# A masked attention loop entered with 14 row products, query spreads in its steps, an earlier self-attention tail, and a front without identity products

## The chip, the cores and the metric

The kernel runs on one core of a Trainium2 chip. The metric is the device time of one execution in microseconds (us). Engines are named as in the profile: PE (TensorE, matrix products and transposes), DVE (VectorE), ACT (ScalarE), POOL (GpSimd) and SP (the queue that issues the DMAs). Every engine works through its own list of instructions in order. An instruction may wait for a semaphore that another engine raises.

## The reference, cut to what matters

Two decoder layers on x of shape (2, 256, 128), each followed by a residual sum and a layernorm. The change touches the first two parts of the second layer: a self-attention with rotary positions (16 heads of 8), and a masked cross-attention to a context of 512 rows (16 heads of 8).

```
x = _layernorm(x + _L0_attn_ref(x, ...))            # state-space mixer
x = _layernorm(x + _L0_xattn_ref(x, ctx_1024, ...)) # cross-attention, 16 heads of 64
x = _layernorm(x + _L0_ffn_ref(x, ...))             # 8 experts
x = _layernorm(x + _L1_attn_ref(x, ...))            # "a" in the kernel
x = _layernorm(x + _L1_xattn_ref(x, ctx_1024, ctx_1024, mask, ...))  # "x" in the kernel
x = _layernorm(x + _L1_ffn_ref(x, ...))             # 32 experts

def _L1_attn_ref(x, ...):
    ...
    attn = jnp.einsum('bhqd,bhkd->bhqk', query, key) / scale
    attn = jax.nn.softmax(attn, axis=-1)
    out = jnp.einsum('bhqk,bhkd->bhqd', attn, value)
    return out.transpose(0, 2, 1, 3).reshape(b, s, d_model) @ Wo_w + Wo_b

def _L1_xattn_ref(query, key_, value, mask, ...):
    ...
    logits = jnp.einsum('bhsd,bhtd->bhst', q, k)
    logits = jnp.where(mask[:, None, :, :], jnp.float32(-100000000.0), logits)
    score = jax.nn.softmax(logits, axis=-1)
    attn = jnp.einsum('bhst,bhtd->bhsd', score, v) / jnp.sqrt(jnp.float32(D_HEAD))
    return jnp.einsum('bhsd,hdo->bso', attn, Wo) + bo
```

## The kernel before

The program is one list per engine, written out by hand with semaphores. The batch has two entries, 0 and 1, of 256 rows. Every attention of layer 1 (`L` is "a" for self-attention, "x" for the masked one) has three pieces.

**Spreads.** Queries and keys are kept as three bf16 parts. A spread is a set of products with a selection matrix (`sel_s`, `sel_k`) that writes the parts of some heads, stacked, into PSUM; ACT copies them to `qs` or `ks`. Its operand is gathered first from the parts by 32-row copies (`gather_four`) on POOL, DVE or ACT; the table `GATHERED` says which engine does which. In "a" there are 16 spreads (`SPREADS`), of keys and queries of both entries, each with 4 products on PE (`spread_a`) and a copy of 128x1024 on ACT. In "x" there are 16 spreads of queries alone (8 per entry), each with 2 products (`spread_x`) and a copy of 128x512 on ACT. The keys of "x" come over DMA.

**The front (`first_slots`, `fill_slot`).** The softmax needs each row's maximum before its exponentials. A row product (`rows`) fills one PSUM bank with 128 query rows by 512 logits; DVE takes the maximum of it (`row_max`), in "x" with the mask in the same instruction. When a group of heads is done, a "max" slot transposes the maxima on PE (`max_cols`), ACT negates them (`minus_max`), POOL splits them in three parts (`minus_parts`) and SP writes these with three DMAs into `qs` (`spread_max`), so that the second set of logits comes out with the maximum already taken off. A slot may only be filled when its bank's slot before it has been read (`before_in_bank`, `used`): a row slot by DVE, a max slot by ACT, that is by `minus_max`. `AHEAD` says how many row products are made before the loop: 16 of 32 for "a", 18 of 64 for "x". `idle_work(bank, n)` makes n products of the identity with itself, whose result nobody reads; `fill_slot` makes 2 ahead of every row product of the front of "a", and 1 in the front of "x".

**The loop.** 16 steps for "a", 32 for "x". In step n PE makes the logits of step n + 1 (`logits`), the products with the values of step n (`values`), and the slots that `slots_beside(L, n)` puts there: up to three row products, or two and a max. ACT takes the exponentials of step n, 128x1024 (`exp_late`). `logits` of a group's first step waits for that group's maxima to have landed (`a_nm_stack`, `x_nm_stack`). In "x" groups are of 4 heads, there are 8 groups, and group k is first needed by the logits of step 4k, which PE makes in step 4k - 1.

**The tail.** For an entry that is finished, PE turns the output to rows (`out_rows`), DVE divides by the sums (`normed_rows`), PE turns back (`attended_cols`) and multiplies by the output weight (`attended_rows`), DVE adds the residual (`a_summed`) and, once POOL has the reciprocal root (`root`), scales (`a_scaled`). The next part starts with a transpose (`half_cols`), the query product of "x" (`queries`) and the split of it (`query_parts`, DVE). `TURNED` and `BESIDE` say in which step of the loop each piece of entry 0 is done; entry 1's come after the loop, or in the front of "x" after the row product named by `SECOND`. Between the loop of "a" and the front of "x" PE goes through `out_rows`, `queries(0)`, `attended_cols(1)`, `attended_rows(1)`, 8 identity products, and `spread_x` 0 and 1, in this order (`attend_x`).

POOL's list around the front of "x" is: the root of post3_0, the gather of entry 0's second quarter, the root of post3_1, the gathers of entry 0's third and fourth quarter, a residual sum, the three gathers of entry 1, and only then `minus_parts("x", 0)` and the others.

## Time and profile before

| | us |
|---|---|
| median of 3 runs | 469.82 |
| lowest, highest | 468.88, 471.14 |
| the profiled execution | 467.58 |
| its span in the trace | 465.8 |
| front of "a" (first row product to first logits) | 33.1 |
| loop of "a", to the copy of its last output | 29.2 |
| from there to the first row maximum of "x" | 6.4 |
| front of "x" | 16.3 |
| loop of "x" | 65.5 |
| rest, to the end | 44.9 |

The last six rows are stretches of the span, cut at 270.4, 303.5, 332.7, 339.1, 355.4 and 420.9 us. The span begins some 2 us after the execution does. A time in the trace is the start of a row, counted from the start of the span. A row of PE's timeline stands for a run of equal products; each product of f32 operands counts as two passes, so that 1 identity product shows as "x2".

### The profile page before, as it was taken

The page shows a single profiled execution, that of the slowest core. Times are in us where ns is not written, and L with a number is a line of the kernel's source. Part 1 is how long each engine was busy: PE and PEld are TensorE (multiplying, and loading weights), DVE is VectorE, ACT ScalarE, POOL GpSimd, SP SyncE. Part 2 cuts the span into 40 slices and gives each one's busy share as a digit, 9 for nine tenths or more (in the row PEclk, how much of TensorE's full clock was granted, in tenths as well). Part 3 has the DMA queues.
Part 4 walks back from the last instruction along what each step waited for, and adds up shares of the span by engine and source line. Part 5 has one row for each costly group of instructions (what it writes and reads, how often), then busy time and mean ns, then how long its engine had stood idle before and what let it go on. Part 6 is the DMA issues. An engine that isn't in the chain of part 4 may idle for free.

```text
span 465.8 us, 7837 instructions
## 1 busy us (share of the span) xinstructions
PE 421.6 (91%) x2952; PEld 283.1 (61%) x2960; DVE 294.9 (63%) x688; ACT 206.2 (44%) x290; POOL 185.9 (40%) x237
## 2 busy tenths in 40 slices
PE   4898989999999999789999986979869999999985
PEld 4686645454545547466899875735546555667975
DVE  4779976767766665532522967555689887246744
ACT  1676623333333332034224364546447444566550
POOL 3326646887777775210222437133154322200000
PEclk9989999999999999899999997989999999999999
DMA  8712000000004111160153015100000000001000
GB/s 287 305 37 77 1 0 2 1 1 0 1 1 180 46 45 46 55 226 0 69 80 45 2 20 69 21 1 4 1 0 3 3 2 3 2 4 32 1 0 24
DMA packets 8081, 19.80 MB, mean 43 GB/s; under 512 B 1958, under 2 KB 3974, under 8 KB 7526
## 3 DMA queue, kind: packets, MB, share of 16 engines
q1 hardware_dynamic: 8044, 19.30, 14.3%
q8 instruction: 24, 0.39, 0.4%
q14 instruction: 13, 0.11, 0.1%
HBM read 17.26 MB, written 1.15 MB: 40 GB/s over the span
## 4 chain that ended last, share of the span: by engine, by line
PE 69%; DVE 15%; issue 5%; POOL 5%; ACT 4%; DMA 1%; another core or an unknown queue 0%; SPq 0%; POOLq 0%; DVEq 0%; ACTq 0%
PE ps L1667 67%; DVE ps L1412 3%; DVE big L1216 2%; POOL big L695 2%; DVE ps L1211 1%; DMA ident<-in_ident 1%; POOL big L702 1%; ACT late L968 1%; DVE big L1288 1%; PE ps L1679 1%; DVE mx_a L1416 1%; POOL big L651 1%; PE ps L2116 1%; ACT big L894 0%; ACT late L1062 0%
## 5 line engine op out<-in xcount | busy, mean ns | idle before, releaser
L1667 PE MATMUL ps<-big,late 128*32 128x256 f32 (+3 forms) x760 | 96.4, 382 | 2.1 <-DVE mx_a L1416 0.9
L1667 PE MATMUL ps<-late,big 128*128 128x128 f32 (+1 forms) x448 | 65.6, 277 | 2.3 <-ACT late L968 1.3
L955 ACT ACTIVATE big<-ps 128x1024 f32<-128x1024 f32 x48 | 49.1, 1024 | 39.0 <-PE ps L1667 38.7
L894 ACT ACTIVATE big<-ps 128x1024 f32<-128x1024 f32 x32 | 32.8, 1024 | 65.2 <-PE ps L1667 56.8
L1667 PEld LDWEIGHTS ps<-late,big 128*128 128x128 f32 (+1 forms) x448 | 47.2, 152 | 20.0 <-issue 13.2
L1667 PEld LDWEIGHTS ps<-big,late 128*32 128x32 f32 (+2 forms) x768 | 35.4, 116 | 38.3 <-issue 18.5
L695 POOL TENSOR_TENSOR big<-big 128x512 f32<-128x512 f32 x32 | 41.0, 1284 | 28.1 <-DVE big L1288 28.1
L1288 DVE TENSOR_SCALAR big<-big 128x1024 f32<-128x1024 f32 x32 | 27.7, 865 | 33.2 <-ACT big L894 33.2
L1412 DVE CUSTOM_DVE_ANT_0 ps<-ps,big 128x512 f32<-128x512 f32 x64 | 42.7, 708 | 6.9 <-remote 3.2
L1667 PE MATMUL ps<-ident 128*128 128x128 f32 x268 | 39.6, 291 | 7.4 <-DMA ident<-in_ident 6.9
L630 POOL TENSOR_SCALAR vareps<-meanvar 128x2 f32<-128x2 f32 (+2 forms) x13 | 3.0, 228 | 104.5 <-DVE meanvar L1110 100.8
L1667 PEld LDWEIGHTS ps<-ident 128*128 128x128 f32 x268 | 36.6, 207 | 8.5 <-DMA ident<-in_ident 6.9
L917 ACT ACTIVATE big<-ps 128x512 f32<-128x512 f32 x32 | 18.9, 598 | 34.0 <-PE ps L1667 34.0
L1667 PE MATMUL ps<-ctx_r,attn_w 128*128 128x512 f32 x64 | 32.6, 618 | 0.7 <-ACT late L861 0.7
L1416 DVE TENSOR_REDUCE mx_a<-ps 128x2 f32<-128x512 f32 x32 | 21.1, 689 | 16.8 <-PE ps L1667 16.7
L1667 PE MATMUL ps<-xT,late 128*128 128x256 f32 (+1 forms) x96 | 29.9, 452 | 1.2 <-ACT big L917 1.2
L1667 PE MATMUL ps<-attn_w,ctx_r 128*128 128x128 f32 (+1 forms) x192 | 29.5, 287 | 0.4 <-ACT late L968 0.3
L1667 PE MATMUL ps<-attn_w,big 128*128 128x128 f32 x192 | 26.5, 285 | 2.9 <-DVE big L1280 2.3
L1279 DVE RECIPROCAL big<-ps 128x256 f32<-128x256 f32 x16 | 28.0, 1748 | 1.3 <-PE ps L1667 1.3
L1667 PEld LDWEIGHTS ps<-attn_w,ctx_r 128*128 128x128 f32 (+1 forms) x192 | 23.7, 171 | 7.4 <-issue 2.8
L651 POOL TENSOR_TENSOR big<-big,mid 128x512 f32<-128x512 f32 x16 | 20.4, 1274 | 19.7 <-DVE big L1216 19.7
L1667 PEld LDWEIGHTS ps<-attn_w,big 128*128 128x128 f32 x192 | 24.3, 197 | 5.9 <-DVE big L1280 2.8
(261 smaller groups left out, 728.3 us busy)
## 6 DMA issues: line engine op xcount, KB each, us to landing
attn_w<-in_w_x SPq DMA_DIRECT2D x1, 2560.0 KB, 12.9
big<-parts_kx SPq DMA_DIRECT2D x18, 128.0 KB
late<-in_w_up SPq DMA_DIRECT2D x1, 2048.0 KB, 8.5
late<-in_w_dn SPq DMA_DIRECT2D x4, 512.0 KB, 4.0
attn_w<-in_w_up SPq DMA_DIRECT2D x1, 1024.0 KB, 7.6
attn_w<-in_w_dn SPq DMA_DIRECT2D x1, 1024.0 KB, 9.8
big<-mid SPq DMA_DIRECT2D x24, 32.0 KB, 1.8
parts_kx<-ctx_r SPq DMA_DIRECT2D x1, 768.0 KB, 3.2
```

The costliest lines, as they stand in the source:

```text
L651: nc.gpsimd.tensor_tensor(hC[:, s % 8, :], hs[:, s % 4, :], Cn[:], ALU.mult).then_inc(S["hC_done"], 1)
L695: nc.gpsimd.tensor_tensor(esum[:, s, :].rearrange("p (r t) -> p r t", r=2), e[:, :, 0, :], e[:, :, 1, :], ALU.add).then_inc(S["e0_sum"], 1)
L702: nc.gpsimd.tensor_tensor(etot[:, b, :], esum[:, 0, :], esum[:, 1, :], ALU.add).then_inc(S["e0_tot"], 1)
L894: nc.scalar.activation(ex[:, n % 3, :].rearrange("p (r n) -> p r n", r=2), ps[:, 2 * (n % 2):2 * (n % 2) + 2, :], ACT.Exp).then_inc(S["e0_ ...
L917: nc.scalar.activation(dst, ps[:, up_bank0(k, c), :], ACT.Gelu).then_inc(S["up0_act"], 1)
L955: nc.scalar.activation(ex1[:, n % 3, :].rearrange("p (r n) -> p r n", r=2), ps[:, 2 * (n % 2):2 * (n % 2) + 2, :], ACT.Exp, scale=scale).t ...
L1216: nc.vector.tensor_tensor_scan(hs[:, s % 4, :], dA[:, s % 2, :], dBx, 0.0, ALU.mult, ALU.add).then_inc(S["scan_done"], 1)
L1279: link(nc.vector.reciprocal(dst, ps[:, 4 + b, T:2 * T]))
L1288: nc.vector.tensor_scalar(ex[:, n % 3, :], ex[:, n % 3, :], float(np.exp(CLIP)), float(np.exp(-CLIP)), ALU.min, ALU.max).then_inc(S["e0_cl ...
L1412: nc.vector.tensor_tensor_reduce(ps[:, bank, :], ps[:, bank, :], mq[:, 2 * b + q, :], 1.0, -FAR, ALU.add, ALU.max, dst).then_inc(S[f"{L}_r ...
L1416: nc.vector.tensor_reduce(dst, ps[:, bank, :].rearrange("p (h k) -> p h k", h=heads), AX.X, ALU.max).then_inc(S[f"{L}_redmax"], 1)
L1667: return nc.tensor.matmul(o, lhsT, rhs, start=start, stop=stop, skip_group_check=shared)
```

## The change

1. `AHEAD["x"]` goes from 18 to 14. Four row products move from the front of "x" into its loop. The max slot of a group is placed after the first row product of the next group, no longer after its second.
2. The 8 spreads of entry 1's queries leave the front of "x". `later_slots` adds one to each of the first 8 steps of the loop, as the last slot of the step. ACT's copy of it comes after the exponentials of the step. `spreads_x` spreads entry 0 beside rows 1, 3, 5, 7, 9 and 11.
3. `BESIDE["x"]` and `TURNED["x"]` come one or two steps later, to follow the row products.
4. Entry 0's tail of "a" comes one step earlier (`TURNED` 9 to 8, "aT" 11 to 10, "y" 12 to 11); its scaling goes from step 15 to step 13, its transpose `half_cols` to step 14 and `queries(0)` to step 15. `query_parts(0)` stands ahead of `normed_rows("a", 1)` on DVE.
5. In the front of "x", `queries(1)` follows row product 4 instead of 3, and `query_parts(1)` follows maximum 8 instead of 5.
6. In the front of "a" identity products go from 48 to 11. Entry 1's spreads are ordered keys first, and spreads 8 to 11 stand together ahead of row product 8. `values_a` comes last.

```diff
-        SPREADS = [(kind, b, f) for b in range(B)
-                   for kind, f in (("k", 0), ("k", 1), ("q", 0), ("k", 2), ("q", 1), ("k", 3), ("q", 2), ("q", 3))]
+        SPREADS = ([(s[0], 0, int(s[1])) for s in ("k0", "k1", "q0", "k2", "q1", "k3", "q2", "q3")]
+                   + [(s[0], 1, int(s[1])) for s in ("k0", "k1", "k2", "k3", "q0", "q1", "q2", "q3")])
...
-        AHEAD = {"a": 16, "x": 18}
+        AHEAD = {"a": 16, "x": 14}
...
-                if L == "x" and m % row_steps(L) == 1 and m > 1:
+                if L == "x" and m % row_steps(L) == 0 and m:
                     slots.append(("max", m // row_steps(L) - 1))
...
+                if L == "x" and n < H // 2:
+                    slots.append((n, ("spread", H // 2 + n)))
...
-        TURNED = {"a": 9, "x": 19}
-        BESIDE = {"a": {"aT": 11, "y": 12}, "x": {"aT": 20, "y": 21, "xT": 24, "router": 25}}
+        TURNED = {"a": 8, "x": 21}
+        BESIDE = {"a": {"aT": 10, "y": 11, "xT": 14}, "x": {"aT": 22, "y": 23, "xT": 25, "router": 26}}
...
-            return [m - 2] if 8 <= m < AHEAD["x"] else [2 + m // 2] if m % 2 else []
+            return [2 + m // 2] if m % 2 and m < H - 4 else []
...
-        SECOND = {"xT": 1, "q": 3, "parts": 5}
+        SECOND = {"xT": 1, "q": 4, "parts": 8}
...
+                    for (kind, i), bank in slots_beside("x", n):
+                        if kind == "spread":
+                            spread_x(i, bank)
...
+                query_parts(0)
                 normed_rows("a", 1, 1.0)
...
-            query_parts(0)
             a_summed(1)
...
                     if slot == ("row", 8):
-                        spread_a(8)
-                        spread_a(9)
-                        idle_work(1, 16)
-                        spread_a(10)
-                    fill_slot("a", slot, bank, 2)
+                        idle_work(2, 8)
+                        for n in (8, 9, 10, 11):
+                            spread_a(n)
+                    fill_slot("a", slot, bank, 1 if slot in (("row", 0), ("row", 1), ("row", 8)) else 0)
...
+                    if n == BESIDE["a"]["xT"]:
+                        half_cols("a", 0)
+                    if n == BESIDE["a"]["xT"] + 1:
+                        queries(0)
```

Three places show what the tables do. The first is PE in the loop of "x", around the max slot of group 1. In the kernel before it is the last slot of the front: `mx_x` is the maxima, `neg_i` the mask product that belongs to the logits, a 128x512 product is a row product, and `fours` gathers are waited for by a spread.

```order
L2039 MATMUL ps<-ident,mx_x 4x128 [waits x_redmax]
L2039 MATMUL ps<-ident,mx_x 4x128
L1667 MATMUL ps<-late,big1 128x256 [waits x_nm_stack0]
L1667 MATMUL ps<-late,big1 128x256
L1667 MATMUL ps<-sel,neg_i 128x256 x2
L1667 MATMUL ps<-late,big1 128x256 x2
L1667 MATMUL ps<-sel,neg_i 128x256 x2
L1667 MATMUL ps<-big1,late 128x512 [waits x_redmax,x_spread]
```

In the changed kernel the same slot stands in step 1, with a spread behind it.

```order
L2046 MATMUL ps<-ident,mx_x 4x128 [waits x_redmax]
L2046 MATMUL ps<-ident,mx_x 4x128
L1672 MATMUL ps<-attn_w,ctx_r 128x256 [waits fours_dve,x_redmax]
L1672 MATMUL ps<-attn_w,ctx_r 128x256
L1672 MATMUL ps<-big2,late 32x256 [waits x_e_exp]
L1672 MATMUL ps<-big2,late 32x256 x3
L1672 MATMUL ps<-big1,late 128x512 [waits x_spread,nm_ps]
L1672 MATMUL ps<-late,big1 128x256 [waits x_e_exp]
```

The row product that opens the next step now waits for `nm_ps` (`minus_max` on ACT); the same holds behind the max slots of groups 2 and 3.

The second place is ACT in the loop of "x", from its first exponentials (128x1024) on. Before:

```order
L955 ACTIVATE big2<-ps 128x1024 [waits x_s_ps] x3
L955 ACTIVATE big2<-ps 128x1024 [waits x_e_used,x_s_ps]
L1012 ACTIVATE mid<-ps 4x256 [waits x_nm_done,x_mT_ps]
L955 ACTIVATE big2<-ps 128x1024 [waits x_e_used,x_s_ps] x3
L1012 ACTIVATE mid<-ps 4x256 [waits x_nm_done,x_mT_ps]
```

And in the changed kernel:

```order
L957 ACTIVATE big2<-ps 128x1024 [waits x_s_ps]
L1005 ACTIVATE late<-ps 128x512 [waits x_spread_ps]
L957 ACTIVATE big2<-ps 128x1024 [waits x_s_ps]
L1005 ACTIVATE late<-ps 128x512 [waits x_spread_ps]
L957 ACTIVATE big2<-ps 128x1024 [waits x_s_ps]
L1014 ACTIVATE mid<-ps 4x256 [waits x_mT_ps]
L1005 ACTIVATE late<-ps 128x512 [waits x_spread_ps]
```

A spread's copy now stands between any two of the first exponentials, and `minus_max` (4x256) behind both.

The third place is DVE at the end of the loop of "a". `COPY mid` keeps an output, `rden` and `x2` are `normed_rows`, `ctx_r`, `cv` and `attn_w` are `query_parts`. Before:

```order
L1442 COPY mid<-ps 128x256 [waits a_e_used,norm_out]
L1425 RECIPROCAL rden<-ps 128x16 [waits a_oT_ps]
L1425 RECIPROCAL rden<-ps 128x16
L1429 SCALAR_TENSOR_TENSOR x2<-ps,rden 128x128 [waits dve_own]
L1429 SCALAR_TENSOR_TENSOR x2<-ps,rden 128x128
L1133 TENSOR_SCALAR ctx_r<-ps,vec 128x256 [waits qk_ps]
```

And in the changed kernel:

```order
L1447 COPY mid<-ps 128x256 [waits a_e_used]
L1138 TENSOR_SCALAR ctx_r<-ps,vec 128x256 [waits qk_ps]
L1140 SCALAR_TENSOR_TENSOR cv<-ps,vec,ctx_r 128x256 [waits x_q_parts]
L1141 CAST ctx_r<-cv 128x256 [waits dve_own]
L1143 TENSOR_TENSOR ctx_r<-cv,ctx_r 128x256 [waits x_q_parts]
L1150 COPY attn_w<-ctx_r 32x256 [waits x_q_parts]
L1150 COPY attn_w<-ctx_r 32x256 x2
L1430 RECIPROCAL rden<-ps 128x16 [waits a_oT_ps]
```

The split of the queries now lies ahead of `normed_rows`, for whose result PE waits before it goes on to the spreads of "x". POOL's and SP's lists are the same in both kernels.

## Rows read from the trace of the kernel before

**Rows 1.** Stretches: PE, PEld, DVE, ACT, POOL; clock, DMA, GB/s.
```profile
270.40:303.50 33.10, 26.59 (x203) 23.35 (x201) 20.48 (x38) 17.03 (x22) 14.45 (x28) 0.90 0.29 39
...
339.10:355.40 16.30, 12.12 (x86) 8.99 (x85) 14.98 (x44) 8.59 (x16) 9.56 (x21) 1.00 0.00 0
355.40:420.90 65.50, 63.25 (x595) 36.12 (x599) 42.16 (x143) 35.75 (x43) 15.63 (x30) 1.00 0.03 9
```
**Rows 2.** PE's timeline in the front of "a": start, duration, [idle before, releaser].
```profile
279.60 0.38 PE L2039 MATMUL ps<-ident,mx_a 128*8 128x128 f32 x2 [0.88 <-DVE mx_a L1416]
...
285.36 1.89 PE L1667 MATMUL ps<-big,ctx_r 96*128 96x256 bf16 x8 [3.89 <-ACT big L945]
287.04 5.10 PE L1667 MATMUL ps<-ident 128*128 128x128 f32 x32
...
303.50 1.86 PE L1667 MATMUL ps<-late,big 128*128 128x256 bf16 x8 [1.31 <-ACT late L968]
```
**Rows 3.** DVE's timeline there: row maxima of "a".
```profile
293.28 1.36 DVE L1416 TENSOR_REDUCE mx_a<-ps 128x2 f32<-128x512 f32 x2 [4.27 <-PE ps L1667]
```
**Rows 4.** POOL's timeline there: the key gathers of entry 1.
```profile
284.07 4.41 POOL L730 COPY big<-ctx_r 32x256 bf16<-32x256 bf16 x9 [1.14 <-DVE ctx_r L1138]
```
**Rows 5.** DVE's timeline at the end of the loop of "a".
```profile
332.30 0.43 DVE L1442 COPY mid<-ps 128x256 f32<-128x256 f32 x1 [0.69 <-PE ps L1667]
333.25 0.37 DVE L1425 RECIPROCAL rden<-ps 128x16 f32<-128x16 f32 x2 [0.53 <-PE ps L2116]
...
334.06 0.48 DVE L1133 TENSOR_SCALAR ctx_r<-ps,vec 128x256 bf16<-128x256 f32 x1
...
335.88 1.02 DVE L1145 COPY attn_w<-ctx_r 32x256 bf16<-32x256 bf16 x3
```
**Rows 6.** PE's timeline there: entry 1's tail, identity products, first spreads of "x".
```profile
334.20 0.44 PE L2125 MATMUL ps<-ident,x 128*128 128x128 f32 x2 [0.50 <-DVE x L1429]
...
335.66 1.95 PE L1667 MATMUL ps<-ident 128*128 128x128 f32 x16
337.44 0.60 PE L1667 MATMUL ps<-attn_w,ctx_r 96*128 96x256 bf16 x4
```
**Rows 7.** POOL's timeline, front of "x": gathers of entry 1's queries.
```profile
346.83 4.05 POOL L730 COPY attn_w<-ctx_r 32x256 bf16<-32x256 bf16 x9 [3.39 <-DVE ctx_r L1138]
```
**Rows 8.** PE's timeline, loop of "x": logits, max slots, a row product.
```profile
355.36 0.38 PE L1667 MATMUL ps<-late,big 128*128 128x256 bf16 x2
...
368.52 0.38 PE L2039 MATMUL ps<-ident,mx_x 128*4 128x128 f32 x2
...
370.06 0.38 PE L1667 MATMUL ps<-big,late 128*128 128x512 bf16 x1
370.28 0.38 PE L1667 MATMUL ps<-late,big 128*128 128x256 bf16 x2
...
375.11 0.38 PE L2039 MATMUL ps<-ident,mx_x 128*4 128x128 f32 x2
```
**Rows 9.** DVE's timeline there: the masked maximum of that row product.
```profile
370.48 0.70 DVE L1412 CUSTOM_DVE_ANT_0 ps<-ps,big 128x512 f32<-128x512 f32 x1
```
**Rows 10.** ACT's timeline: a spread's copy, exponentials and `minus_max`, step after step.
```profile
355.33 0.60 ACT L1003 ACTIVATE late<-ps 128x512 bf16<-128x512 f32 x1 [0.43 <-PE ps L1667]
...
362.13 1.02 ACT L955 ACTIVATE big<-ps 128x1024 f32<-128x1024 f32 x1 [1.17 <-PE ps L1667]
363.05 0.36 ACT L1012 ACTIVATE mid<-ps 4x256 f32<-4x256 f32 x1
```
**Rows 11.** ACT's last `minus_max` of "a", and PE's wait for its DMA.
```profile
320.79 0.36 ACT L1012 ACTIVATE mid<-ps 8x256 f32<-8x256 f32 x1
```
**Rows 12.** PE's timeline: the logits that wait for it.
```profile
325.46 0.60 PE L1667 MATMUL ps<-late,big 128*128 128x256 bf16 x4 [0.33 <-DMA late<-mid]
```
**Rows 13.** Two stretches, columns as in Rows 1.
```profile
283.00:290.00 7.00, 4.64 (x23) 4.21 (x24) 5.68 (x14) 3.37 (x5) 5.19 (x13) 0.51 0.55 70
344.50:351.30 6.80, 4.15 (x31) 3.07 (x32) 6.61 (x20) 3.45 (x7) 3.90 (x10) 1.00 0.00 0
```

More of the change, by code:

```diff
@@ L984, in attend_a @@
                 gather_four(1)
-                for n in range(8, 15):
+                for n in range(8, 16):
                     spread(n)
                 minus_max("a", 1, dict(first_banks("a"))["max", 1])
-                spread(15)
                 for n in range(B * (H // 4) * KEYS["a"] // P):
@@ L2016, in used @@
                     pe.wait_ge(S[f"{L}_redmax"], i + 1)
+                elif kind == "spread":
+                    pe.wait_ge(S["x_spread"], i + 1)
                 else:
@@ L2064, in fill_slot @@
                     rows(L, i, bank)
+                elif kind == "spread":
+                    spread_x(i, bank)
                 else:
@@ L2173, in attend_a @@
                         spread_a(7)
+                    if slot == ("row", 6):
                         front_products(1)
@@ L2176, in attend_a @@
                         latent_products(1)
-                    if slot == ("row", 9):
-                        spread_a(11)
-                    if slot == ("row", 11):
-                        spread_a(12)
-                    if slot == ("row", 13):
-                        spread_a(13)
-                        values_a()
-                    if slot == ("row", 15):
-                        spread_a(14)
+                    if slot in (("row", 9), ("row", 11), ("row", 13)):
+                        spread_a(12 + (slot[1] - 9) // 2)
                 spread_a(15)
+                values_a()
                 for slot, bank in slots_beside("a", None)[-2:]:
@@ L2202, in attend_a @@
                         out_rows("a", 1, range(H // 4 - 1))
+                    if n == BESIDE["a"]["xT"]:
+                        half_cols("a", 0)
+                    if n == BESIDE["a"]["xT"] + 1:
+                        queries(0)
                     values("a", n)
@@ L2209, in attend_x @@
                 total = B * (H // 4) * KEYS["x"] // P
-                half_cols("a", 0)
                 out_rows("a", 1, (H // 4 - 1,))
-                queries(0)
                 attended_cols("a", 1)
```

5 lines of the change are left out of this document (2 added, 3 removed).

## The prediction, made before the changed kernel was run

> **What bounds the kernel now.** I read four views: the stretches of the span with each engine's busy time, the timelines of PE, DVE, ACT and POOL where the change works, the waits with their releasers, and the order of the instructions. The stretches [rows 1] show two kinds of place. In the loop of "x" PE is busy 63.25 of 65.5 us, so whatever is put in PE's list there is paid in full, and every new wait too. In the two fronts PE is busy 80% and 74%. What sets their length is read from the timelines: chains through DVE, ACT and POOL, and in "a" also the identity products. Nothing ahead of 270 us or behind the loop of "x" is touched, so the four stretches between carry the whole sum.
>
> **Front of "a": shorter by 7.3 us.** PE reaches the first max slot at 279.60 [rows 2]. The 16 identity products ahead of it cost 3.5 us of PE. DVE needs 8 maxima at 0.65 (1.36 for two that overlap a little, [rows 3]), the scaling of entry 1's x (0.6), and a wait for row product 7 behind `front_products` (some 0.9), which makes 6.7 from 271.1. The slot comes 1.9 us earlier, at 277.7. From there to 285.36 the chain runs through the key split and ACT's gather (the 3.89 of idle time, [rows 2]), and it moves along by 1.9: spread 8 starts at 283.4. The 8 identity products now lie in PE's idle time and cost nothing; without that cover they would cost 1.8. Spreads 9 to 11 wait for POOL's key gathers, 4.41 for the three [rows 4], which end at 288.5 now and at 286.6 then. Row product 8 goes out at 287.2 and DVE starts on it at 287.65, where it starts at 293.28 now [rows 3]; before, 16 identity products ran from 287.04 to 291.98 [rows 2]. Eight maxima take 5.2, to 292.9. Then come the max slot, spread 15, `values_a` (1.1) and DVE's addition of it (0.7): first logits at 295.4 where they are at 303.50 [rows 2], 8.1 less. I take 7.3. The reason is the clock: from 283 to 290 the granted clock is 0.51, the level of 1.2 GHz, after a stretch with PE idle for 3.9 us; from 344.5 to 351.3 it is full with PE busy 61% [rows 13]. [...] At the low level a pair of row products and a spread costs PE 1.76, not 0.88, against DVE's 1.3; that is 0.46 for each of four pairs. Bounds: 6.0 and 8.1.
>
> **The tail: longer by 3.0 us.** Step 8 still waits for the last `minus_max` of "a" and the logits of step 12 for its DMA [rows 11, 12], so the earlier `out_rows` moves little. `half_cols(0)` stands in step 14 and waits for the scaling, some 0.4 of wait; ACT copies it ahead of the exponentials of step 15, and the values of step 15 end 0.65 late. The last output is kept at 333.4, not at 332.73 [rows 5]. Then DVE does `query_parts(0)` and its gather first, 334.06 to 336.90 or 2.84 [rows 5], and only then `normed_rows`, after which PE starts `attended_cols(1)` 0.95 later (333.25 to 334.20, [rows 5, 6]). That gives 337.2 where it is 334.20. The earlier split gains nothing, since in PE's list the spreads of "x" stand behind this transpose. All behind it moves by 3.0: the identity products at 335.66, the first spreads at 337.44 [rows 6].
>
> **Front of "x": longer by 1.8 us.** It has fewer products, but they are not what ends it. POOL's gathers of entry 1's queries end at 350.88 [rows 7], and `minus_parts("x", 0)` is behind them. From the end of a `minus_max` to the logits that need it are 4.31 (321.15 to 325.46, [rows 11, 12]), so 350.88 gives 355.19, and the first logits are at 355.36 [rows 8]. With `query_parts(1)` behind maximum 8 instead of 5, POOL starts three maxima, 2.0, later. The slack of 0.2 is used up, and 1.8 is left. The four row products, 8 spreads and the max slot that leave this front were beside that chain; their removal is worth nothing here.
>
> **Loop of "x": longer by 10.9 us.** Three steps take 6.59 (368.52 to 375.11), one 2.20; a row product takes 0.22 of issue (370.06 to 370.28, [rows 8]). Of the 2.20, row products are 0.66, logits 0.88 and the rest, the values, 0.66.
> - A step with three row products and a spread: the spread uses bank 7, where the second row product went. That is issued at 0.66, DVE starts 0.42 later (370.06 to 370.48) and takes 0.70 [rows 8, 9], so the spread is issued at 1.85 and not at 1.54. With 0.22 and 0.66 behind it the step is 2.73, or 0.53 more. Five such steps: 2.7. Lower bound: the 0.22 of issue alone, 1.1.
> - A step with a max slot (1, 4 and 7): the slot uses bank 6, and the next step opens with a row product in bank 6, which waits for `minus_max`. ACT takes the spread's copy first (0.60), from 2.27 to 2.87, then exponentials (0.92 until the next may start) and `minus_max` (0.36) [rows 10]: 4.15 from the step's start, and the row product at 4.2, not at 2.2. Three times 2.0 is 6.0. Before, the waiting row product was the second of its step and no spread's copy stood ahead of the exponentials.
> - Group 1's maxima are needed by the logits of step 4, made in step 3. `minus_max` ends at 4.15 of step 1, plus 4.31 makes 8.5; PE is there at 4.2 + 2.73 + 0.22 = 7.15. Another 1.3.
> - The four row products from the front land in steps that had none: 0.9.
>
> Together 10.9. No row shows a spread inside this loop, so both ends stay: 2.7 if only the issue is paid (8 spreads and 4 row products at 0.22), 12 if values and DVE slip too.
>
> **Clock at the two new gaps: 1.2 us longer.** PE is idle from 333.7 to 337.2 ahead of `attended_cols(1)`, and some 4 us ahead of the first logits of "x" (counted from the first maximum of "x": the last one ends at 13.9, after 7.8 for the first nine, 2.8 for the split and its gather and 3.3 for five more; the logits are at 16.3 + 1.8 = 18.1). The nearest row is the gap of 3.89 before 285.36, after which the clock stayed at 0.51 until 290 [rows 2, 13]. If both fall, the 8 identity products and the entry of the loop run at half speed and cost up to 5; if neither, nothing. The Trainium skill (TensorE: Matmul & The Clock Gate, "What's actually happening") states that the throttled clock is the default and that activity releases it; by that rule, which the 0.51 behind the gap agrees with, taking identity products out of a sparse front is no free gain. It is the rival below and not in this sum.
>
> **The sum.** -7.3 + 3.0 + 1.8 + 10.9 + 1.2 = +9.6. The profiled execution took 467.58, which gives 477.2. The median of the three runs is 2.2 above it, and the forecast goes by the median: 469.8 + 9.6 = 479.4. The forecast's own range: -8.1, +3.0, +1.6, +8.3 and 0 at the low end, 474.6; -6.0, +3.2, +2.0, +12 and +5 at the high end, 486.
>
> **Rivals.** (1) The clock stays low: the front of "a" saves 5, the 8 identity products cost 1.8 more, and the masked loop's entry 2.5 more. With 3.0, 1.8, 10.9 and 0.9 for the max steps that run partly at half speed the sum is about +15, 485. For it: the two low stretches of this trace, each behind a sparse stretch. Against: 344.5 to 351.3 stayed full. (2) The waits in the masked loop cost half, because ACT is ahead there (idle 1.17 before each exponential, [rows 10]) and takes copies sooner: +5.5 instead of +10.9, -8.1 in front, no clock cost, +2.2, 472.0. (3) Faster: `minus_max` is done before the next row product needs its bank. That decides between 0.66 after the max slot (no wait) and the 2.8 that I count. Then the loop costs 2.7, the front saves 8.1, the low clock at the entry of the loop of "a" goes too (1.6), and the tail and the front of "x" still cost 4.8: -2.2, 467.6. Against it stands ACT's own list, in which the copy of the step's spread and the exponentials are ahead. (4) The front of "a" does not shorten as told, since it waits for POOL's gathers: it saves 4, and the time is 483.
>
> **How the numbers follow.** Chances: forecast 0.64, rival 1 0.16, rival 2 0.09, rival 3 0.06, rival 4 0.05. The predicted time is the forecast's, 479.4. The range 471.5 to 486 takes in the forecast's own range, rivals 1 and 4, and rival 2. A measurement of this kernel can tell about 0.5% from no change, 2.3 us. Faster (below 467.5): 0.04, half of rival 3 and a little. Same: 0.07, the rest of rival 3 and half of rival 2. Slower: 0.89.
>
> **What would show it.** First logits of "a" some 7 to 8 us earlier in the span; `attended_cols(1)` with a long wait for DVE and `query_parts(0)` ahead of it; first logits of "x" 18 us after the first masked maximum, not 16.3; in the first 8 steps of the masked loop a PE timeline with three waits of 1.5 to 2 us on `minus_max` and one on a DMA, 27 to 28 us for the 8 steps instead of 17.6; the granted clock under 1 in at least one more stretch. The prediction fails if PE meets no `nm_ps` wait there, or if the identity products that went had kept the clock up.

## The result, and the profile after

The changed kernel takes 479.99 us (median of 4 runs, 477.43 to 480.71), the kernel before 470.48 in the same comparison (468.88 to 471.32). The ratio is 1.0196, 95% interval 1.0148 to 1.0245: slower by 9.5 us, where 479.4 was forecast. The profiled execution took 479.72. The one of the kernel before took 467.58, 2.9 under the median here, so the two traces stand 12.1 us apart and the medians 9.5. Three executions of the whole study fell into a slow state (480.69 us of the kernel with `minus_max` first, 707.03 of the one with the split back behind `normed_rows`, 1059.26 of the kernel before) and are in none of the medians or ratios.

The page of the changed kernel, its head, the busy times and the granted clock in 40 slices:

```profile
span 477.9 us, 7691 instructions
...
PE 418.8 (88%) x2870; PEld 273.5 (57%) x2878; DVE 294.5 (62%) x688; ACT 205.1 (43%) x290; POOL 185.6 (39%) x237
...
PEclk9999999999999999899999988998959999999998
```

PE does 2.8 us less and the span is 12.1 us longer. The time is in waits. The three stretches that answer to [rows 1] (same columns), front of "a", front of "x", loop of "x":

```profile
269.70:296.50 26.80, 20.54 (x128) 13.69 (x127) 20.00 (x38) 16.95 (x22) 13.87 (x28) 0.87 0.31 47
337.30:354.60 17.30, 9.22 (x55) 6.52 (x53) 12.54 (x37) 4.34 (x8) 7.71 (x17) 0.83 0.00 1
354.60:434.70 80.10, 71.23 (x623) 40.03 (x630) 45.78 (x153) 39.77 (x51) 15.58 (x30) 0.97 0.03 7
```

The last stretch runs to the transpose of the routing weights (434.67). Counted to the same transpose (422.51) before the change it is 67.2 us long, so it grew by 12.9.

**Front of "a".** PE's timeline (start, duration, [idle before, releaser]): max slot 0, spread 8, row product 8, max slot 1, first logits. [Rows 2] has the same places.

```profile
277.00 0.38 PE L2046 MATMUL ps<-ident,mx_a 128*8 128x128 f32 x2 [0.87 <-DVE mx_a L1421]
...
282.77 1.16 PE L1672 MATMUL ps<-big,ctx_r 96*128 96x256 bf16 x8 [1.91 <-ACT big L947]
...
287.19 1.06 PE L1672 MATMUL ps<-big,late 128*128 128x256 bf16 x4
...
293.66 0.38 PE L2046 MATMUL ps<-ident,mx_a 128*8 128x128 f32 x2 [0.89 <-DVE mx_a L1421]
...
296.51 1.03 PE L1672 MATMUL ps<-late,big 128*128 128x256 bf16 x8 [0.94 <-DVE late L1476]
```

The first logits are 7.0 us earlier. Of this 0.7 was there before the front began (its first product is at 269.7, not 270.4), 1.9 falls ahead of the first max slot and 4.4 behind it: 6.3 net.

**The loop of "a".** One wait in it is longer than before: the logits of step 12 wait 1.89 us for their DMA, where it was 0.33 [rows 12].

```profile
319.05 0.60 PE L1672 MATMUL ps<-late,big 128*128 128x256 bf16 x4 [1.89 <-DMA late<-mid]
```

Nine of the traced kernels have the moved steps of the tail. In three of them (the changed kernel and the two in the section on the tail) this wait is 1.64 to 1.89 us, in the other six none is recorded. In the five kernels without the moved steps it is 0.32 or 0.33. So it is a matter of the execution; whether the moved steps make it likelier is not shown.

**The tail.** DVE keeps the last output, splits entry 0's queries, gathers, and only then takes up `normed_rows` (the reciprocal). PE's two rows are `attended_cols(1)` and the 8 identity products.

```profile
326.76 0.42 DVE L1447 COPY mid<-ps 128x256 f32<-128x256 f32 x1 [2.37 <-PE ps L1672]
327.11 0.47 DVE L1138 TENSOR_SCALAR ctx_r<-ps,vec 128x256 bf16<-128x256 f32 x1
...
328.92 1.02 DVE L1150 COPY attn_w<-ctx_r 32x256 bf16<-32x256 bf16 x3
329.97 0.37 DVE L1430 RECIPROCAL rden<-ps 128x16 f32<-128x16 f32 x2
```
```profile
330.92 0.44 PE L2134 MATMUL ps<-ident,x 128*128 128x128 f32 x2 [3.24 <-DVE x L1434]
...
332.85 2.97 PE L1672 MATMUL ps<-ident 128*128 128x128 f32 x16
```

PE stands still for 3.24 us, where it was 0.50 [rows 6], and the identity products behind take 2.97, not 1.95. DVE's reciprocal starts 3.21 behind the copy of the last output (326.76 to 329.97), where it was 0.95 (332.30 to 333.25, [rows 5]): 2.26 more. The copy itself is late too. From the last max slot of "a" to it are 12.33 us before the change (319.97 to 332.30) and 13.20 in the trace of the tail alone and in those of five other kernels that have the moved steps and no late DMA: 0.87 more. (The changed kernel needs 14.98, with 1.78 for the late DMA.)

**Front and loop of "x".** PE's timeline: the first logits; the max slot of step 1; the row product of bank 6 that opens step 2 (its row carries the name of the logits); the logits of group 1; the spreads of steps 5 and 6.

```profile
354.64 0.61 PE L1672 MATMUL ps<-late,big 128*128 128x256 bf16 x2 [3.03 <-DMA late<-mid]
...
361.44 0.38 PE L2046 MATMUL ps<-ident,mx_x 128*4 128x128 f32 x2
...
364.48 0.38 PE L1672 MATMUL ps<-late,big 128*128 128x256 bf16 x2 [1.50 <-ACT mid L1014]
...
368.34 0.38 PE L1672 MATMUL ps<-late,big 128*128 128x256 bf16 x2 [0.91 <-DMA late<-mid]
...
376.96 0.39 PE L1672 MATMUL ps<-attn_w,ctx_r 96*128 96x256 bf16 x2 [0.20 <-DVE mx_x L1417]
...
379.75 0.39 PE L1672 MATMUL ps<-attn_w,ctx_r 96*128 96x256 bf16 x2 [0.20 <-DVE mx_x L1417]
```

The 1.50 on `mid` is the wait for `minus_max`; it stands again at 375.30 and 385.01. From the max slot to the row product behind it are 3.04 us (361.44 to 364.48). A step with three row products and a spread takes 2.79 (376.96 to 379.75). The first eight steps take 28.7 (356.32 to 385.01). ACT's timeline beside the first of the three waits: the spread's copy, the exponentials, and `minus_max` behind both, ready to run since the max slot at 361.44:

```profile
362.44 0.60 ACT L1005 ACTIVATE late<-ps 128x512 bf16<-128x512 f32 x1 [1.41 <-PE ps L1672]
362.94 1.02 ACT L957 ACTIVATE big<-ps 128x1024 f32<-128x1024 f32 x1
363.84 0.36 ACT L1014 ACTIVATE mid<-ps 4x256 f32<-4x256 f32 x1
```

### The profile page after: what moved, and what is told of

Its sections match the earlier page's. It is cut to its first block, busy times and chain, and to the rows that moved or that the text cites. A ratio compares the mean times of both kernels' runs of the same rounds, so it can differ in the third digit from the quotient of the medians.

```text
span 477.9 us, 7691 instructions
## 1 busy us (share of the span) xinstructions
PE 418.8 (88%) x2870; PEld 273.5 (57%) x2878; DVE 294.5 (62%) x688; ACT 205.1 (43%) x290; POOL 185.6 (39%) x237
## 4 chain that ended last, share of the span: by engine, by line
PE 61%; DVE 15%; POOL 7%; issue 6%; ACT 5%; DMA 3%; SPq 1%; another core or an unknown queue 1%; POOLq 0%; DVEq 0%; ACTq 0%
PE ps L1672 59%; DVE ps L1417 3%; POOL big L697 2%; DVE mx_a L1421 1%; DMA late<-mid 1%; DVE big L1221 1%; SPq L560 1%; DVE ps L1216 1%; DMA big<-mid 1%; DVE big L1293 1%; POOL big L732 1%; POOL big L704 1%; POOL attn_w L732 1%; DMA ident<-in_ident 1%
## 5 line engine op out<-in xcount | busy, mean ns | idle before, releaser
L1672 PE MATMUL ps<-big,late 128*32 128x256 f32 (+3 forms) x760 | 97.5, 383 | 2.9 <-DVE mx_a L1421 1.8
L1672 PE MATMUL ps<-ident 128*128 128x128 f32 x186 | 29.0, 307 | 9.5 <-DMA ident<-in_ident 5.7
L1672 PEld LDWEIGHTS ps<-ident 128*128 128x128 f32 x186 | 27.4, 222 | 10.5 <-DMA ident<-in_ident 5.7
L744 POOL CAST mid<-mid 4x256 bf16<-4x256 f32 (+1 forms) x12 | 4.6, 387 | 64.5 <-ACT mid L1014 64.4
L1672 PE MATMUL ps<-attn_w,big 128*128 128x128 f32 x192 | 25.5, 279 | 2.9 <-DVE big L1285 2.3
L1672 PEld LDWEIGHTS ps<-attn_w,ctx_r 128*128 128x128 f32 (+1 forms) x192 | 22.0, 162 | 10.6 <-DVE mx_x L1417 4.0
L1672 PE MATMUL ps<-big,mid 64*128 64x256 f32 x192 | 27.2, 402 | 0.0
## 6 DMA issues: line engine op xcount, KB each, us to landing
attn_w<-in_w_x SPq DMA_DIRECT2D x1, 2560.0 KB, 12.9
```

Of the source, the lines that this page charges most:

```text
L1672: return nc.tensor.matmul(o, lhsT, rhs, start=start, stop=stop, skip_group_check=shared)
```

## Each part of the change alone

Three kernels hold one part each. They and the fourth kernel were timed beside the kernel before, whose median was 470.76 (19 runs). The others were timed in two later sessions, in which it was 469.9 (22 runs) and 470.04 (17 runs). A ratio is always to the kernel before in the same session. It need not agree with the difference of two medians to better than 1 or 2 us, and where the two differ both are given.

The front of "a" alone. Its diff against the kernel before, cut:

```diff
-                        spread_a(8)
-                        spread_a(9)
-                        idle_work(1, 16)
-                        spread_a(10)
-                    fill_slot("a", slot, bank, 2)
+                        idle_work(2, 8)
+                        for n in (8, 9, 10, 11):
+                            spread_a(n)
+                    fill_slot("a", slot, bank, 1 if slot in (("row", 0), ("row", 1), ("row", 8)) else 0)
```

> The kernel before with only the new front of "a" (entry 1's key spreads first, no identity products ahead of rows 2 to 7 and 9 to 15, values_a last). Theory (the front's length is that of DVE's maxima, ACT's gather and POOL's gathers once the identity products are gone, 6.3 net in the trace of after): 6.3 us faster than before, about 464, with the first logits of "a" 7.0 us earlier in the span. Rival (most of it is given back in the loop of "a", whose DMA and exponentials set its end): 3 us faster or less.

Measured: 462.96 us, ratio 0.9845 (0.9808 to 0.9882), 7.8 us faster by the medians and 7.3 by the ratio. In its trace the first logits are at 297.35, 6.15 before those of [rows 2], and the span is 6.3 shorter. Nothing is given back behind them, so the rival falls.

The tail alone:

```diff
-        TURNED = {"a": 9, "x": 19}
+        TURNED = {"a": 8, "x": 19}
...
-        BESIDE = {"a": {"aT": 11, "y": 12}, "x": ...
+        BESIDE = {"a": {"aT": 10, "y": 11, "xT": 14}, "x": ...
...
+                query_parts(0)
                 normed_rows("a", 1, 1.0)
```

> The kernel before with only entry 0's tail moved one or two steps forward in the loop of "a" and its queries' split ahead of normed_rows on DVE. Theory (PE waits for normed_rows, which is 2.84 us later): 3 us slower than before, up to 4.5 with a low clock behind the longer gap; the transpose attended_cols(1) waits 3 us for DVE. Rival (the earlier split of the queries lets the front of "x" begin earlier, and what it costs on DVE it gives back): within 1 us of before.

Measured: 472.86 us, ratio 1.0059 (1.0035 to 1.0083), 2.1 us slower by the medians and 2.8 by the ratio. PE's `attended_cols(1)`:

```profile
337.63 0.44 PE L2126 MATMUL ps<-ident,x 128*128 128x128 f32 x2 [3.25 <-DVE x L1430]
```

The masked loop alone:

```diff
-        AHEAD = {"a": 16, "x": 18}
+        AHEAD = {"a": 16, "x": 14}
...
+                if L == "x" and n < H // 2:
+                    slots.append((n, ("spread", H // 2 + n)))
...
-        SECOND = {"xT": 1, "q": 3, "parts": 5}
+        SECOND = {"xT": 1, "q": 4, "parts": 8}
```

> The kernel before with only the masked loop's change (14 rows ahead of it, entry 1's query spreads in its first eight steps, queries(1) behind row 4, query_parts(1) behind maximum 8). Theory (PE is the bound there and gets 8 slots, three waits of 1.5 us and a DMA wait into its list, and the split comes three maxima later): 12 us slower than before, 11.7 from the loop and 1.1 from the front, less some 1 us if the clock stays full at the entry of the loop. Rival (part of the 12.7 in the trace of after comes from the low clock that the changed front and tail brought): 7 to 8 us slower.

Measured: 483.11 us, ratio 1.0271 (1.0237 to 1.0304), 12.4 us slower. The same waits are there without the new front and tail (the second row is the wait for group 1's maxima):

```profile
367.41 0.38 PE L1672 MATMUL ps<-late,big 128*128 128x256 bf16 x2 [1.50 <-ACT mid L1014]
...
371.29 0.38 PE L1672 MATMUL ps<-late,big 128*128 128x256 bf16 x2 [0.93 <-DMA late<-mid]
```

The rival falls as well: with the old front and tail the masked loop is 79.9 us long in the trace, and its entry is at the low clock all the same (0.59 from 357.8 to 361.8).

By the medians the three parts give -7.8 + 2.1 + 12.4 = +6.7, and together they measure +9.5. By the ratios they give -7.3 + 2.8 + 12.7 = +8.2, against +9.2. Each interval is 1 to 2 us either way, so the parts add as far as these runs can tell; whether they cost a little more together stays open.

## The masked loop: which wait, and why

ACT's order in the first eight masked steps, against the changed kernel:

```diff
-                    for (kind, i), bank in slots_beside("x", n - 1) if n else ():
+                    for (kind, i), bank in slots_beside("x", n - 1) if n > H // 2 else ():
                         if kind == "max":
                             minus_max("x", i, bank)
-                    for (kind, i), bank in slots_beside("x", n):
+                    for (kind, i), bank in slots_beside("x", n) if n < H // 2 else ():
+                        if kind == "max":
+                            minus_max("x", i, bank)
                         if kind == "spread":
                             spread_x(i, bank)
```

> The changed kernel, where ACT in the first eight masked steps takes minus_max of the step's max slot ahead of the copy of its spread and of the next exponentials, not behind both. Theory (the row product that opens the next step waits for minus_max behind those two): the three waits of 1.5 us go, 4.5 to 5 us faster than the changed kernel, about 475. Rival (ACT is as late with the exponentials instead, and PE waits for them): at most 1.5 us faster.

Measured: 474.6 us (8 runs), ratio to the kernel before 1.0087 (1.0054 to 1.012), 5.4 us faster than the changed kernel. ACT takes `minus_max` first, and PE's next wait is 0.16. The loop, first logits to the routing transpose, is 75.3 us, not 80.0. ACT and then PE at step 1:

```profile
359.62 0.37 ACT L1014 ACTIVATE mid<-ps 4x256 f32<-4x256 f32 x1 [0.78 <-PE ps L2048]
360.21 0.60 ACT L1005 ACTIVATE late<-ps 128x512 bf16<-128x512 f32 x1 [0.22 <-PE ps L1674]
360.70 1.02 ACT L957 ACTIVATE big<-ps 128x1024 f32<-128x1024 f32 x1
```
```profile
359.20 0.38 PE L2048 MATMUL ps<-ident,mx_x 128*4 128x128 f32 x2
...
360.90 0.38 PE L1674 MATMUL ps<-late,big 128*128 128x256 bf16 x2 [0.16 <-ACT late L1005]
...
364.15 0.38 PE L1674 MATMUL ps<-late,big 128*128 128x256 bf16 x2 [0.30 <-DMA late<-mid]
```

The exponentials lose nothing by it: they start 1.50 behind the max slot in both kernels (361.44 to 362.94, 359.20 to 360.70). The rival falls.

The spreads back in the front, still with 14 rows ahead:

```diff
-                if L == "x" and n < H // 2:
-                    slots.append((n, ("spread", H // 2 + n)))
...
-            return [2 + m // 2] if m % 2 and m < H - 4 else []
+            return {8: [6], 9: [7], 10: [8], 11: [9], 12: [10, 11], 13: [12, 13, 14, 15]}.get(m, [2 + m // 2] if m % 2 else [])
```

> The changed kernel with entry 1's query spreads back in the front of "x" (behind rows 8 to 13), still 14 rows ahead of the loop. Theory (the spreads lengthen five steps by 0.6 and, by the bank that they take, make the next step open with a row product that waits 1.5 us for minus_max, three times): 3.7 + 4.5 in the loop, less 1.3 that a longer wait for the DMA of group 1's maxima takes and 1 for the spreads in the front: 6 us faster than the changed kernel, 474. Rival (it is the four rows and the late max slots that cost, whoever else is in the step): at most 3 us faster.

Measured: 471.9 us, ratio 1.0057 (1.0022 to 1.0092), 8.1 us faster than the changed kernel by the medians, 6.5 by the ratios. The loop is 70.8 us. Its first logits, and those of group 1:

```profile
354.91 0.39 PE L1670 MATMUL ps<-late,big 128*128 128x256 bf16 x2 [0.20 <-DMA late<-mid]
...
364.93 0.38 PE L1670 MATMUL ps<-late,big 128*128 128x256 bf16 x2 [2.16 <-DMA late<-mid]
```

The spreads lie in what was the wait ahead of the first logits (0.20 here, 3.03 in the changed kernel). So of the 12.9 us that the loop grew, 9.2 go with the spreads (80.0 less 70.8). Not all of this is slots and waits: the entry of the loop is at full clock here (1.00 from 354.9 to 358.9) and at 0.50 in the changed kernel, and that costs 1.8, as the kernel with filled gaps below shows (78.2 against 80.0). The slots and waits that the spreads bring are thus 7.4. Of the 3.7 that are left the longest piece is the wait for group 1's maxima, which grew from 0.91 to 2.16 because PE reaches it sooner.

The front of "x" takes 17.39 us with the 8 spreads back in it and 17.36 without them (first masked maximum to first logits). Taking them out gained nothing there.

## The front of "x"

`queries(1)` and `query_parts(1)` as early as before, in the changed kernel:

```diff
-        SECOND = {"xT": 1, "q": 4, "parts": 8}
+        SECOND = {"xT": 1, "q": 3, "parts": 5}
```

> The changed kernel with queries(1) behind row 3 and query_parts(1) behind maximum 5, as before. Theory (POOL's gathers and minus_parts end the front of "x"): the first logits come 2 us earlier after the first masked maximum, 15.4 instead of 17.4, and the time is 478. Rival (the low clock or the wait for DVE's maximum ahead of row 12 ends the front): no change.

Measured: 480.33 us, ratio 1.0246 (1.0207 to 1.0285): 0.3 slower than the changed kernel by the medians and 2.3 by the ratios, with intervals that overlap. No gain is seen. Max slot 0 and the first logits:

```profile
349.69 0.38 PE L2046 MATMUL ps<-ident,mx_x 128*4 128x128 f32 x2 [3.48 <-DVE mx_x L1417]
...
355.37 0.61 PE L1672 MATMUL ps<-late,big 128*128 128x256 bf16 x2 [0.26 <-DMA late<-mid]
```

From `attended_cols(1)` to the first logits this trace needs 21.76 us (333.61 to 355.37), the changed kernel's 23.72 (330.92 to 354.64). So the 2.0 us are gained in the stretch, as the theory says, though the wait moves from the DMA to the max slot. The time doesn't show it. In the two profiled executions this kernel's first max slot of "a" is at 279.14, 2.1 us behind the changed kernel's 277.00, in a part where their instructions are the same, and its first logits of "a" wait 2.16 for a DMA, where the changed kernel's wait 0.94 for DVE. The trace bears the step out; the runs don't resolve it.

## The tail: order or steps

`query_parts(0)` back behind `normed_rows`, the moved steps kept:

```diff
-                query_parts(0)
                 normed_rows("a", 1, 1.0)
...
             attend_a()
+            query_parts(0)
             a_summed(1)
```

> The changed kernel with query_parts(0) back behind normed_rows of entry 1 on DVE; out_rows, attended_cols, half_cols and queries of entry 0 stay one or two steps forward. Tells DVE's order from the steps moved. Theory (normed_rows waits 2.84 us for the split and its gather, and nothing else of the tail costs): 2.8 us faster than the changed kernel, about 477, the wait ahead of attended_cols(1) falls from 3.24 us to about 0.5. Rival (the moved steps cost in the loop of "a" and the split is hidden): less than 1 us faster.

Measured: 477.0 us (4 runs), ratio 1.0137 (1.0106 to 1.0168), 3.0 us faster than the changed kernel by the medians and 2.8 by the ratios. DVE's reciprocal comes ahead of the split, and PE's wait is 0.98 (not 0.5: `queries(0)` filled the other half of it before, and now stands in the loop):

```profile
329.18 0.37 DVE L1430 RECIPROCAL rden<-ps 128x16 f32<-128x16 f32 x2 [0.53 <-PE ps L2125]
...
329.99 0.47 DVE L1138 TENSOR_SCALAR ctx_r<-ps,vec 128x256 bf16<-128x256 f32 x1
```
```profile
330.13 0.44 PE L2134 MATMUL ps<-ident,x 128*128 128x128 f32 x2 [0.98 <-DVE x L1434]
```

The steps moved forward, beside the new front of "a" and with DVE's old order. Against the kernel with that front alone, cut:

```diff
-        TURNED = {"a": 9, "x": 19}
+        TURNED = {"a": 8, "x": 19}
...
-        BESIDE = {"a": {"aT": 11, "y": 12}, "x": ...
+        BESIDE = {"a": {"aT": 10, "y": 11, "xT": 14}, "x": ...
...
+                    if n == BESIDE["a"]["xT"]:
+                        half_cols("a", 0)
+                    if n == BESIDE["a"]["xT"] + 1:
+                        queries(0)
```

> The kernel before with the new front of "a" and entry 0's steps moved forward, but with the split of the queries behind normed_rows (e1 and the half of e2 that is not DVE's order). Theory (the moved steps are neither late nor early for anyone, since PE's spreads stand behind attended_cols(1)): as e1, 463. Rival 1 (half_cols and queries out of the tail take 1 us off it): 462. Rival 2 (the wait for the scaling in the loop is paid): 464.

Measured: 463.41 us, ratio 0.9862 (0.9835 to 0.9889), against 462.96 and 0.9845 without them. The larger part of the tail's cost is DVE's order. That the moved steps cost nothing is not shown: the runs have 0.5 to 0.8, and in every trace that has them the last output of "a" is kept at least 0.87 late. The two rivals, 1 us to either side, can't be told from the theory by these runs.

## The front of "a": order, identity products, clock

The new order with two identity products ahead of every row product:

```diff
-                    fill_slot("a", slot, bank, 1 if slot in (("row", 0), ("row", 1), ("row", 8)) else 0)
+                    fill_slot("a", slot, bank, 2)
```

> The new front of "a" alone (as in e1), but with the two identity products ahead of every row product, as the kernel before has them. Tells the new order from the products that went. Theory (DVE's maxima at 0.65 set the pace of the second half, where two products a row are hidden; in the first half 12 products more cost 3.0 less 0.9 of idle time, some 2): 2 us slower than e1, 465; the order and the 16 products ahead of row 8 make the rest of the gain, some 5. Rival 1 (identity products cost as issued): 5 us slower than e1, near 468. Rival 2 (they keep the clock up, and its low stretches behind the gap go): as fast as e1 or 1 us faster.

Measured: 465.23 us, ratio 0.9942 (0.9909 to 0.9975), 2.3 slower than the front alone by the medians and 4.5 by the ratios. Its 12 runs fall in two groups, eight from 464.7 to 467.0 and four from 468.7 to 469.5; the profiled execution is of the second. In it max slot 0 is 2.1 later than in the front alone (279.75 against 277.67), max slot 1 is 5.8 later (299.74 against 293.98). Of the first, 1.9 is the 2 that was expected, and 0.2 was there before the front began. The other 3.7 were expected to be hidden. A part of the stretch between (columns as in [rows 1]):

```profile
288.70:295.00 6.30, 6.30 (x31) 5.48 (x32) 2.39 (x5) 2.73 (x3) 3.56 (x9) 0.52 0.32 48
```

PE is busy all of it, nearly all at the level of 1.2 GHz, so the products that hide beside DVE at full clock are paid here. Rival 2 falls: the identity products did not keep the clock up. Counted to the first logits, the front is 5.0 us longer (1.9 ahead of max slot 0 and 3.15 behind it), which is rival 1's size.

The whole span is 7.3 longer, and one piece of it is no cost of these products. The front of "x", which this kernel leaves as it was, takes 19.45 us against 16.28 in the front alone; its mean granted clock is 0.82 there, against 1.00. So the two groups of runs can't be read as theory and rival. A fairer comparison takes runs with the same mean granted clock of the whole execution: at 0.983 this kernel took 464.7 to 465.3 and the front alone 461.3, at 0.977 it took 468.7 to 469.5 and the front alone 462.8 to 465.6. With the 4.5 of the ratios, that speaks for rival 1 more than for the theory.

The gap ahead of spread 8 filled, in the kernel with the front of "a" alone:

```diff
-                        idle_work(2, 8)
+                        idle_work(2, 15)
                         for n in (8, 9, 10, 11):
```

> The new front of "a" alone (as e1) with 15 identity products ahead of spread 8 in place of 8, which fill most of the 1.91 us that PE waits there for ACT's gather. Theory (the low clock of the 3 to 4 us behind comes of PE standing still, and costs some 1.5 us there and at the entry of the loop of "a"): 1 to 2 us faster than e1, 461.5. Rival (DVE and POOL set this stretch, or the clock falls all the same): as e1, 463, or 0.5 slower.

Measured: 461.49 us, ratio 0.982 (0.9797 to 0.9843), against 462.96 and an interval that overlaps. It has the lowest median of the study. Max slot 0, spread 8 and first logits, here and then in the front alone:

```profile
275.58 0.38 PE L2038 MATMUL ps<-ident,mx_a 128*8 128x128 f32 x2 [0.88 <-DVE mx_a L1415]
...
281.34 1.15 PE L1666 MATMUL ps<-big,ctx_r 96*128 96x256 bf16 x8 [0.35 <-ACT big L945]
...
294.69 1.67 PE L1666 MATMUL ps<-late,big 128*128 128x256 bf16 x8 [0.94 <-DVE late L1470]
```
```profile
277.67 0.38 PE L2038 MATMUL ps<-ident,mx_a 128*8 128x128 f32 x2 [0.88 <-DVE mx_a L1415]
...
283.44 1.15 PE L1666 MATMUL ps<-big,ctx_r 96*128 96x256 bf16 x8 [1.91 <-ACT big L945]
...
297.35 1.87 PE L1666 MATMUL ps<-late,big 128*128 128x256 bf16 x8 [1.47 <-DMA late<-mid]
```

From max slot 0 to spread 8 both need 5.8 us: the products fill the gap and cost nothing. To the first logits it is 19.1 against 19.7. The clock still falls behind the gap (0.62 from 283.9 to 287.2). So 0.6 us is what the traces show in the front, and the rest of the 1.5 is not told apart from chance: all four runs have a mean granted clock of 0.983 or 0.984 and took 461.0 to 461.8, and the two runs of the front alone with 0.98 or more took 461.3 and 461.6.

## The clock at the two gaps

12 identity products ahead of `attended_cols(1)` and 12 ahead of the first logits of "x", in the changed kernel:

```diff
+                idle_work(2, 12)
                 attended_cols("a", 1)
...
+                idle_work(0, 12)
                 logits("x", 0)
```

> The changed kernel with 12 identity products (some 3 us at full clock) ahead of attended_cols(1), and 12 ahead of the first logits of "x", where PE waits for DVE and for a DMA. Theory (the gaps bring the granted clock to 0.5 for some 3 to 7 us behind them, which costs 1.4 at the tail and 2 at the entry of the masked loop): both low stretches go, 3 us faster than the changed kernel, about 477. Rival (what runs behind the gaps at half speed waits for DVE and ACT anyway): no change, or up to 1 us slower for products that don't fit in the gaps.

Measured: 478.27 us (475.14 to 481.11), ratio 1.0206 (1.0162 to 1.025) against the changed kernel's 1.0196: no difference can be told. The two stretches behind the gaps in the changed kernel, then in this one:

```profile
331.60:335.00 3.40, 3.17 (x15) 3.17 (x16) 1.16 (x5) 0.18 (x1) 0.43 (x2) 0.50 0.00 0
348.80:358.80 10.00, 6.01 (x23) 3.91 (x25) 3.48 (x10) 1.02 (x1) 3.67 (x8) 0.50 0.00 1
```
```profile
329.20:333.00 3.80, 3.33 (x28) 3.04 (x28) 1.16 (x5) 0.59 (x2) 0.73 (x2) 1.00 0.00 0
345.50:355.50 10.00, 7.34 (x59) 5.76 (x62) 4.35 (x14) 1.76 (x3) 3.84 (x9) 1.00 0.00 1
```

In the profiled execution the theory holds for the clock: the granted clock is 1.00 in both, the identity products behind the first gap take 1.95 again, and the loop is 78.2 us long, not 80.0. That execution is also the fastest of the six. The other five are as slow as the changed kernel, though the mean granted clock is higher in all six (0.976 to 0.987) than in the changed kernel's four (0.965 to 0.975). So the filled gaps raised the clock every time, and what that is worth in time is not shown; without a trace of the five it stays open. The Trainium skill (TensorE: Matmul & The Clock Gate, "What's actually happening") says that the throttled state is the default and that activity releases it. The one trace, with 1.00 behind both filled gaps, agrees.

## The changed kernel mended

`minus_max` first, entry 1's split early in the front of "x", entry 0's behind `normed_rows` in the tail. The diff is that of the fourth kernel with these lines:

```diff
-        SECOND = {"xT": 1, "q": 4, "parts": 8}
+        SECOND = {"xT": 1, "q": 3, "parts": 5}
...
-                query_parts(0)
                 normed_rows("a", 1, 1.0)
...
             attend_a()
+            query_parts(0)
```

> The changed kernel with three mends at once: minus_max ahead of the spread's copy (e4), queries(1) and query_parts(1) early (e7), and query_parts(0) behind normed_rows (e9). Theory (the three costs lie one behind the other and add): 5.3 + 2.0 + 2.8, so 10 us faster than the changed kernel, about 470, as the kernel before and 7 slower than e1. Rival (they overlap, or the wait for the first masked max slot and the low clock take the gain of e7): 473.

Measured: 469.25 us, ratio 0.9991 (0.9965 to 1.0017), 10.7 us faster than the changed kernel, as the theory said. The three mends one by one measured 5.4, -0.3 and 3.0, or 8.1; the sum of 10 needs the 2.0 that only the trace of the early split shows. So the costs add within the noise, and no closer. The masked loop as it is meant, with its worst waits gone (74.7 us), still takes back all that the front of "a" gains.

## Why the prediction was right, step by step

- **Front of "a", forecast -7.3:** right in mechanism, a little large. The trace has -6.3 net of an earlier start, the part alone -7.8 by the medians and -7.3 by the ratio. From max slot 0 to spread 8 it is 5.8 us (5.7 forecast), to row product 8 10.2 (9.5), from there to max slot 1 6.5 (some 5.8 at full clock) and on to the first logits 2.85 (some 2.4). That row product 8 stands at 287.19, with 287.2 forecast, is luck: the execution was 0.7 ahead. The four slow pairs at 0.46 add up to 1.8, and the forecast took 0.8 without saying why. Measured are 1.8 over its 17.7 at full clock, but at most 0.7 of that lies where those pairs are; the rest is in the pieces ahead of and behind them.
- **The tail, +3.0:** right in cause and size. Up to `attended_cols(1)` the tail's own cost is 3.13 in the traces: 0.87 for the moved steps (0.65 forecast) and 2.26 for the split ahead of `normed_rows`. The forecast's 2.84 is the whole split, but DVE had stood idle for 0.53 ahead of the reciprocal [rows 5], and that time takes up a part of it. The part alone costs 2.1 to 2.8, and undoing the order gives back 2.8 to 3.0.
- **Front of "x", +1.8:** right in cause; the stretch grew by 1.1 (16.30 to 17.36), and an early split brings 2.0 in the trace. The forecast took a chain that ends at POOL's last gather plus 4.31; that is what the trace has (350.57 to 354.64, 4.07). That the spreads taken out are worth nothing there is shown by putting them back.
- **Loop of "x", +10.9:** right. The trace has +12.9, and +11.1 when the clock is full at its entry (78.2 against 67.2). Its pieces: steps of 2.79 (forecast 2.73), three waits for `minus_max` of 1.50 behind exactly the instructions named (3.04 from max slot to row product, 2.8 forecast, and 0.66 by rival 3), and a wait of 0.91 for group 1's maxima (1.3). The eight steps take 28.7, of which 1.8 is the clock (27 to 28 forecast). Rival 3, that `minus_max` is done in time, is what the fourth kernel builds by hand; it does not come by itself.
- **Clock, +1.2:** the identity products at the tail took 1.02 longer and the loop 1.8, 2.8 in all; both gaps fell low, where the forecast gave each a part. Against this stands a gain that only rival 3 had counted: the entry of the loop of "a", at 0.51 before the change, is at full clock here, and from the first logits to the next max slot are 7.74 us, not 8.94. Net this is 1.6 in the profiled execution. Over the runs the size is not known, since filling the gaps did not move the median beyond the noise.
- **The sum:** the terms of the trace are -0.7 -6.3, +3.7 from the first logits of "a" to `attended_cols(1)` (3.1 for the tail, 1.8 for the late DMA, which no term had, and -1.2 for the clock), +2.6 from there to the first logits of "x", +12.9 in the loop: 12.2 against 12.1 of span. The mechanisms were right, but that +9.6 met the medians' 9.5 to 0.1 is luck. In the traces the same sum is 2.5 short, and the profiled execution of before was a fast one, 2.9 under its median. Rival 1 adds up to 15.9 from its own terms, not to 15.

## What to carry to other kernels

A slot added to a loop whose engine is the bound costs its issue, and often more by what it does to the turn of the banks: ask for each buffer which instruction frees it, and what stands ahead of that instruction on its engine. Here a 0.36 us copy behind two longer ones made PE wait three times 1.5 us, and putting it ahead of them gave these 4.5 back. Work that an engine does early for a later stage must not stand ahead of what its neighbour waits for now, and work taken out of a stretch is worth something only where that stretch's end hangs on it.

## What was not expected of the hardware

The times of one kernel spread more than was thought when the bounds were set: the kernel before ran from 466.6 to 472.8 us on one chip, where the three runs at the start lay within 2.3. In the traces the same unchanged instructions ahead of the front of "a" end up to 2 us apart (the first max slot is at 275.58 and at 277.67 in two kernels that are equal up to there), and which stretches behind it fall to the granted clock of 0.50 differs.

The record shows how much of this goes with the clock. Of the kernel before, the five runs with a mean granted clock of 0.983 took 466.6 to 466.9 us, and those with 0.973 took 470.7 to 472.8. In the traces of the kernels with the new front of "a" (without the added identity products), two stretches of untouched work, at 30 and at 195 us, account for most of the difference in its first max slot. Where neither falls to 0.50, the slot is at 275.58 and 275.81; where only the second does, at 277.00, 277.04 and 278.09; where both do, at 277.6 to 277.8; where the second stays at 0.50 for some 7 us and not 3.5, it is at 279.14. Why they fall in one execution and not in the next is not shown.

A single profile is thus one of several. A step of under 2 us is read from the distance between two rows of one stretch, with its granted clock beside it, and not from the span; runs are best compared at the same mean clock.
